# Recurrent stage and first attention tiles as one written order on each engine

## What is computed

```python
# block 1, in chunks of 64 tokens, 4 heads; state S runs over the chunks
q, k, v = x @ Wq, x @ Wk, x @ Wv
g = log_sigmoid(x @ Wgk1 @ Wgk2 + bgk2) / 16
b = cumsum(g)                        # within the chunk
A = tril((q * exp(b) * scale) @ (k * exp(-b)).T)
o = A @ v + (q * exp(b) * scale) @ S
S = S * exp(b_last) + (k * exp(b_last - b)).T @ v
y = (rmsnorm(o) * silu(x @ Wg)) @ Wo
# block 2, for each of 2 layers, 8 heads of 64, windows of 64 with one window back
q, k, v = split(shift(x) @ wqkv)
q, k = rotary(l2norm(q)), rotary(l2norm(k))
x = x + local_attention(q, k, v) @ wo
a, h = split(layernorm(shift(x)) @ w1 + b1)
x = x + (a * gelu(h)) @ w2 + b2
```

## Time and profile before

| what | value |
|---|---|
| median of 3 runs | 436.88 us (436.65 to 438.52) |
| profiled execution, device time | 436.81 us |
| its span (first to last instruction) | 435.0 us |
| busy: PE, DVE, ACT, POOL | 408.1, 338.7, 305.8, 292.5 us |
| granted TensorE clock, mean | 0.998 |

### The profile page before, as it was taken

The page is one execution under the profiler, slowest core; times in us unless marked ns, Lnnn a source line. Parts: engine busy times, 40 slices in busy tenths (PEclk is TensorE's granted clock), DMA queues, the critical chain, the costliest instruction groups (busy, mean ns, idle before and its releaser), DMA issues.

```text
span 435.0 us, 13205 instructions
## 1 busy us (share of the span) xinstructions
PE 408.1 (94%) x4851; PEld 291.9 (67%) x4851; DVE 338.7 (78%) x715; ACT 305.8 (70%) x684; POOL 292.5 (67%) x288
## 2 busy tenths in 40 slices
PE   3898999879999999999999999999999999999994
PEld 2566666656776877777765666777777777766563
DVE  2678867889988989989845277799899899855676
ACT  3677768757887887887773346778878888876324
POOL 3578967799978778777722536667767767761425
PEclk9999999999999999999999999999999999999999
DMA  7830000000000000000000000000000000000012
GB/s 188 313 91 3 2 3 3 3 1 2 8 14 10 9 10 11 8 8 14 8 9 13 0 2 1 7 10 8 11 11 8 8 15 9 8 8 12 8 36 62
DMA packets 21055, 10.37 MB, mean 24 GB/s; under 512 B 13253, under 2 KB 20225, under 8 KB 20993
## 3 DMA queue, kind: packets, MB, share of 16 engines
q1 hardware_dynamic: 20272, 9.08, 7.6%
q10 hardware_dynamic: 720, 0.46, 0.4%
HBM read 6.38 MB, written 1.05 MB: 17 GB/s over the span
## 4 chain that ended last, share of the span: by engine, by line
PE 66%; issue 7%; POOL 6%; ACT 5%; DVE 4%; POOLq 0%; ACTq 0%; DVEq 0%
PE psum L640 49%; PE psum L912 6%; PE psum L954 5%; PE psum L979 4%; ACT sq L1380 1%; PE psum L885 1%; ACT probs_t L1412 1%; POOL ping L446 1%; DVE o_n L1999 1%; POOL qr L475 1%; POOL qr L483 1%; ACT qk_t L1399 1%; DVE neg_max L1972 1%; PE psum L999 1%; POOL zn L511 1%
## 5 line engine op out<-in xcount | busy, mean ns | idle before, releaser
L475 POOL TENSOR_TENSOR qr<-rot 128x1024 f32<-128x1024 f32 x32 | 75.8, 2370 | 27.0 <-DVE rot L1944 22.2
L640 PE MATMUL psum<-wqkv_sb,h_t 128*128 128x512 f32 x192 | 93.0, 594 | 0.0
L483 POOL TENSOR_TENSOR qr<-qr,inv 128x1024 f32<-128x1024 f32 x32 | 60.9, 1902 | 33.6 <-ACT inv L1391 33.6
L1952 DVE TENSOR_REDUCE ss<-sq 128x16 f32<-128x1024 f32 x32 | 39.0, 1218 | 14.9 <-ACT sq L1380 14.7
L1405 ACT ACTIVATE probs<-probs 128x512 f32<-128x512 f32 x64 | 39.4, 631 | 13.8 <-DVE probs L1979 13.5
L1972 DVE TENSOR_REDUCE neg_max<-psum 128x4 f32<-128x512 f32 x64 | 41.5, 685 | 7.1 <-PE psum L640 5.7
L640 PE MATMUL psum<-z_t,w_sb 128*128 128x512 f32 (+1 forms) x96 | 44.7, 595 | 0.0
L640 PEld LDWEIGHTS psum<-wqkv_sb,h_t 128*128 128x128 f32 x192 | 31.7, 191 | 16.3 <-issue 16.2
L1979 DVE TENSOR_TENSOR probs<-psum,neg_max 128x512 f32<-128x512 f32 x64 | 41.3, 681 | 0.2
L1944 DVE TENSOR_TENSOR rot<-psum,cos_t 128x1024 f32<-128x1024 f32 x32 | 39.1, 1222 | 2.7 <-PE psum L640 2.4
L640 PEld LDWEIGHTS psum<-v_mix,probs_t 128*64 128x64 f32 x512 | 32.2, 137 | 12.7 <-issue 11.1
(11 more groups left out here) (155 smaller groups left out, 967.0 us busy)
## 6 DMA issues: line engine op xcount, KB each, us to landing
wqkv_sb<-in_L_ffn_wqkv SPq DMA_DIRECT2D x1, 1536.0 KB, 10.0
hcat<-middle SPq DMA_DIRECT2D x32, 32.0 KB
hcat<-middle SPq DMA_DIRECT2D x32, 31.8 KB
out_x<-pong SPq DMA_DIRECT2D x7, 128.0 KB, 1.8
x_in<-in_L_attn_x SPq DMA_DIRECT2D x2, 384.0 KB, 4.9
w_sb<-in_L_ffn_w SPq DMA_DIRECT2D x1, 682.0 KB
cos_base<-rotary_cos SPq DMA_DIRECT2D x1, 512.0 KB, 5.5
sin_base<-rotary_sin SPq DMA_DIRECT2D x1, 512.0 KB, 6.7
```

Source lines behind the costliest of these rows:

```text
L475: pool.tensor_tensor(o, a, b[:, :, ::-1, :], ALU.add).then_inc(s["add_ready"], 1)
L483: pool.tensor_tensor(a, a, inv[:, :].unsqueeze(2).to_broadcast([P, 2 * AH, DH]), ALU.mult).then_inc(s["qr_ready"], 1)
L640: return pe.matmul(o, w, m, start=start, stop=stop, skip_group_check=skip)
L1952: dve.tensor_reduce(ss[:, 0:4 * AH:2], sq[:, :].rearrange("p (h e) -> p h e", e=DH), AX.X, ALU.add).then_inc(s["ss_ready"], 1)
```

## The change

The loop `gla_step` is gone on all four compute engines, with `paired` and `FREE_PAIR`. One written list, `recurrent_stage_and_first_tiles`, holds everything from pair 0 up to where `attn_step` takes over at tile 3. Beside it:

- The combined gate weight is made in bank 7. `transpose_x(0)` no longer waits for its copy, `project_gate(0)` does.
- Pairs 0 and 1 are normalised on VectorE (`normalise_first`), not on GpSimd; pair 0 between the two copies of gate weights.
- The transposed o goes to bank 3, with one copy of 512 columns. `project_vg(t)` waits for the copy of o of pair t-2, `transpose_o(t)` for the reads of v and gate of pair t+1; `intra_outputs` no longer waits for that copy.
- Wgk1 and Wgk2 are loaded from ScalarE's queue, ahead of Wq and Wk; Wv and Wg from SP's, where the former two stood.
- The waits for `d_cols` and `zero_pool` stand in VectorE's list right before `rotate(0)`, in ScalarE's right before `copy_h_t(0)`.

```diff
@@ sync
-            sp.dma_start(wgk1_sb[:, :], Wgk1).then_inc(d["d_low"], 16)
-            sp.dma_start(wgk2_sb[0:RANK, :], Wgk2).then_inc(d["d_low"], 16)
+            sp.dma_start(wvg_sb[:, 0:GV], Wv).then_inc(d["d_vg"], 16)
+            sp.dma_start(wvg_sb[:, GV:2 * GV], Wg).then_inc(d["d_vg"], 16)
@@ tensor
-                pe.transpose(b_xg[0:RANK, 0:P], wgk1_sb[:, :], ident).then_inc(s["w1t_done"], 1)
+                pe.transpose(bank[7][0:RANK, 0:P], wgk1_sb[:, :], ident).then_inc(s["w1t_done"], 1)
                 pe.wait_ge(s["w1t_ready"], 1)
-                mm(b_xg[:, P:2 * P], wgk1_t[0:RANK, :], wgk2_sb[0:RANK, :]).then_inc(s["wgk_done"], 1)
+                mm(bank[7][:, P:2 * P], wgk1_t[0:RANK, :], wgk2_sb[0:RANK, :]).then_inc(s["wgk_done"], 1)
...
                 wait(pe, s["gin_ready"], t)
+                wait(pe, s["ogt_ready"], t - 1)
                 if t == 0:
                     pe.wait_ge(d["d_vg"], 2 * 16)
...
                 wait(pe, s["og1_ready"], t)
-                wait(pe, s["ogt_ready"], t)
...
                 wait(pe, s["og2_ready"], t + 1)
+                wait(pe, s["v_ready"], min(t + 2, NP))
+                wait(pe, s["gin_ready"], min(t + 2, NP))
                 for i in range(2 * B):
-                    ins = pe.transpose(bank[6 + i // 2][:, HC + i % 2 * P:HC + (i % 2 + 1) * P],
+                    ins = pe.transpose(bank[3][:, i * P:(i + 1) * P],
@@ vector
+            def normalise_first(t):
+
+                dve.wait_ge(s["x_rstd"], t + 1)
+                for b in range(B):
+                    at = t * B + b
+                    ins = dve.tensor_scalar(xn[:, at * P:(at + 1) * P], tile_of(x_in, at), mv_x[:, 2 * at:2 * at + 1],
+                                            rstd_x[:, at:at + 1], ALU.subtract, ALU.mult)
+                ins.then_inc(s["xn_ready"], 1)
+
             def copy_gate_weights():
 
                 dve.wait_ge(s["w1t_done"], 1)
-                dve.tensor_copy(wgk1_t[0:RANK, :], b_xg[0:RANK, 0:P]).then_inc(s["w1t_ready"], 1)
+                dve.tensor_copy(wgk1_t[0:RANK, :], bank[7][0:RANK, 0:P]).then_inc(s["w1t_ready"], 1)
+                normalise_first(0)
                 dve.wait_ge(s["wgk_done"], 1)
```

669 lines of the change are left out of this document (427 added, 242 removed).

## The result

| | before | after |
|---|---|---|
| median, same session (4 runs each) | 437.70 us (436.65 to 438.81) | 433.20 us (432.42 to 433.38) |
| profiled execution, device time | 436.81 us | 433.38 us |
| its span | 435.0 us | 431.3 us |

The ratio is 0.9888, 95% interval 0.9843 to 0.9932; timed again in another session (433.18 against 436.96 us) it is 0.9895, 0.9841 to 0.9949: about 1% less time, clear of the noise. The forecast was 433.4 us, counted from the earlier median of 436.88. Some executions of most of these kernels, the one before too, run 2 to 5 us longer at a lower granted clock (mean 0.985 to 0.994 instead of 0.995 to 0.999), which lifts some of the medians, so the gain is read from the spans (3.7 us) and such a trace is compared only in the steps before its clock falls.

The account below looks back on a forecast made before the run. TensorE's own work bounds it from 120.77 us on; before, its 16.6 us idle is all to win. A walk of the lists summed terms to 3.75, less 0.35 allowance: 3.4, so 433.4 us; 8 in 10: 430.6 to 436.9.

Parts of the forecast that it names:

- Start: Up to the first x transposition: it starts near 6.95 us instead of 7.32, +0.4, bounds 0 and 0.6.
- First two pairs: Up to vg(2): gate(1) and vg(1) fill TensorE's wait for pair 0's decays, +1.3 us.
- Pair 2: vg(2) to vg(3): costs 9.4 us, of which 0.65 for casts ahead of decay_q(2); gain 0.7.
- Pair 3: vg(3) to vg(4): costs 9.2 us, with 0.45 for second_state(3) behind decay_log(4); gain 0.4.
- Pairs 4 and 5: vg(4) to scores(6): each pair costs 8.75 us, gains 0.5 and 0.4.
- bank 3 ring: vg, copy and gate_input, o transposition, copy: 4.4 us in a pair of 8.75, hidden, free until 4 us late.
- Last pairs to the first tile: scores(6) to project_qk(0) +0.1, to transpose_qk(0) +0.35, to tile 3's scores -0.4; allowance for forgotten hand-offs -0.35 us.
- GpSimd did not hold TensorE: Rival: gate_o(7) late on GpSimd holds transpose_o(7) at tile 0, 439.1 us and more; 0.10 including other stalls.
- Waits moved: Waits for column transfers cost nothing at old or new places; the slower table is there at 17.6 us, hidden by 3.5.
- The path of o: Rival: state outputs to transpose_o has no slack, 0.45 us late in six pairs takes 2.7; 436.1 us, chance 0.16.
- The scans: Rival: all eight VectorE scans at their worst, 1.209 us, lose up to 3.0 us; 436.4 us, chance 0.06.
- More than I credit: Rival: each pair costs 8.75 us and the last stretch's five waits vanish, 2 to 3 us more; 431 us, chance 0.06.

Follow-up runs that it names:

- start undone: Changed kernel with weight queues as before, combined gate weight in bank 0, pairs 0 and 1 normalised on GpSimd; 434.43 us against 436.75 before, ratio 0.9936.
- the old order: Changed kernel, bank 3 and start edits kept, with pairs 0 to 3 in the old loop's order; 443.02 us against 436.75 before, ratio 1.0117.
- The moves above: Changed kernel with copy_h_t(2) ahead of gate_exp(7), 433.07 us; also with pair 2's scan ahead of scale_o(0) and row_reciprocals(1), normalise_o(1) ahead of row_max(2), 433.77 us.
- the mixtures tried here: Changed kernel with the old loop's order for pairs 0 to 3, 443.02 us; changed kernel with transposed o back in banks 6 and 7, 451.49 us.
- scan-first: Changed kernel with VectorE's scan of pair 2 ahead of scale_o(0); first run 432.49 us, timed 433.32 us beside 433.18 for the changed kernel.

## Why the prediction was right, and where its terms were wrong

**What bounds the kernel** was right: from tile 3's scores to the end nothing changed, and the 16.6 us of idle TensorE ahead of it were all that could be won. 3.64 of them were. The sum of the terms was forecast as 3.4, but it came right in part by luck: the start gave 1.0 us more than said and the first two pairs 0.9 less, pair 2 gave 0.6 more and pair 3 gave 0.4 less.

**Start, +0.4: mis-sized, 1.39 measured at its landmark.** The part that I had given a price (bank 7, VectorE's normalisation) gave 0.52. What I had left out stands in the trace of the kernel before, TensorE's first instruction:

```profile
5.32 0.37 PE L650 MATMUL psum<-consts,wgk_sb 128*16 128x128 f32 x1 [5.32 <-DMA wgk_sb<-in_L_attn_Wgk]
```

Its wait ended with the low-rank weights (issued from 2.11 us on by SP, now from 0.73 by ScalarE), not with the identity, and moving them was worth 0.87. I had the queue as a risk (a bound of 0), not as a gain. Wv and Wg are first used at 8.11, not after 9, and nothing waited for them.

**First two pairs, +1.3: mis-sized, 0.39.** The order did what I said, and TensorE was 1.4 us ahead of my walk at scores(0) and scores(1) (20.61 against 22.0). Then came 0.43 for copy_kd(1), which I had at 0.5, and the nameless 0.80 (by my reading the instruction block), which no walk over data dependencies shows. From scores(1) to vg(2) my walk had 6.6 us, 6.1 without its wait; measured are 7.89, 6.66 without the waits, so I had also summed the work of this piece 0.5 us too short. The two terms together were 1.7, measured 1.78: the sum was right by luck of two errors, and the experiments show that the two are linked. The start's gain is passed on in part only: 0.93 of 1.18 between the changed kernel and the one with the start undone (whose first x transposition is at 7.11), and nothing of 0.79 in the second execution of the same kernel.

**Pair 2, +0.7: 1.34.** The pair took 8.79 us; the 0.65 that I charged for the casts did not come. Their price was wrong: the earlier trace rows show the masks' cast at 1.424, but that is behind the start of a GpSimd product; here it started 0.02 us ahead of second_state(1) and took 0.35, while second_state(1) took 0.58 instead of 0.40. The scan made up for this, however: scan and casts took 2.31 us, not far below the 2.46 that I had reckoned (0.84, 1.42 and 0.2). What failed is the path. TensorE, held up in key_values(1), gave the outputs of pair 1 late, so that behind the casts VectorE had to wait for square_o(1),

```profile
28.31 0.69 DVE L1902 TENSOR_REDUCE o_ss<-z_t 128x8 f32<-128x512 f32 x1 [0.52 <-ACT z_t L1331]
```

and gate_input(2) was done at 31.80, before TensorE was free for transpose_o(1) at 31.91. With the scan moved, scan and casts took 2.58 us and the pair 8.84.

The Trainium skill, page "SBUF — State Buffer", section "SBUF: two separate sides", says that a GpSimd instruction and a VectorE instruction that uses both ports or has two SBUF inputs exclude each other for a whole instruction, and that the one that starts first goes first. The traces agree: 0.05 us behind gate_o(0) the scan took 1.75 us (0.69 when moved away), and 0.03 behind it the identity's cast took 1.32 (0.21), each ending within 0.6 us of gate_o's end.

**Pair 3, +0.4: -0.02.** I had 0.45 for second_state(3) standing behind decay_log(4); the wait is there, 0.73, but the cause that I named is wrong. GpSimd was free 0.32 us before second_state(3) started; its input came late, out of key_values(3) over state_0(3), and it took 0.71 instead of 0.40 beside VectorE's scan. Swapping it with decay_log(4) takes away the second part and costs more in the next pair, as far as one run tells.

**Pairs 4 and 5, +0.5 and +0.4: 0.44 and 0.14.** Pair 4 takes 8.78 with no wait; pair 5 has 0.26 before project_gate, for the copy of x. That the bank 3 ring is hidden was right for the new order, where no wait for it shows, but my margin of 4 us was not a property of the ring: in the old order the same ring costs 5.8 us in four places.

**Last pairs to the first tile, +0.1, +0.35, -0.4, allowance -0.35: 0.05, 0.15, -0.24.** The waits of the walk are there: 1.07 before transpose_in(3), 0.44 and 0.77 later ones, and transpose_o(7) waits only 0.17 for gate_o(7), so GpSimd did not hold TensorE. The moves above show for two of them, the 1.07 and the 0.77, that they are not gains left lying: each has a second condition close behind.

**Waits moved, 0: right** (1.0006). The tables were in time as well: cos in 5.0 us, sin in 6.2, and no wait of GpSimd on them.

**Rivals.** The path of o did not take the gain: no wait of TensorE on gate_o in each pair. The scans were worse at their worst than my bound (1.755), but their median fell (0.839 to 0.781), and VectorE's busy time ahead of tile 3 rose by 2.4 us (90.63 to 93.01), of which 1.2 are the four normalisations that it took over, so the kernel was not held by it. "More than I credit" was held off by the nameless wait in the start and by 0.73 in pair 3.

## What to carry to other kernels

Price an instruction by its row only after seeing what ran beside it on GpSimd or VectorE: the masks' cast was 1.42, 0.57 and 0.35 us here, the identity's 0.21, 0.73 and 1.32, and second_state 0.71 and 0.40. A buffer's place and the order around it are one decision: either half of this change without the other made the kernel 6 to 15 us slower, in the mixtures tried here. Before blaming the instruction ahead in an in-order list, look whether the engine idles behind it: then it is the input that is late. Before moving an instruction to remove a wait, look for the condition that ends next, on the engine that waits and on the one that gives up its filler.

## What the runs showed of the hardware that was not expected

- TensorE stands still for 0.53 to 1.63 us at one place of its instruction stream while the weights are still loading, and goes on 2.5 to 2.8 us after a 16 KB packet starts on the queue "q8 instruction" (ten traces; that the one causes the other is inferred). An earlier start of the kernel can be lost there entirely (0.79 us in one trace). What sets the start of the packet (20.75 to 22.85) stays open, and so does whether the packet is slowed by the weights.
- The granted clock falls after some of these waits and not after others. In two traces in which TensorE goes on at 25.37 and 25.43, after waits of 1.13 and 1.14, the page's clock is lower in the third of its 40 slices and vg(2) starts at 31.30 and 31.36; it doesn't fall where TensorE goes on at 25.61 after 0.81 (start undone), nor after the longest wait, 1.63. Windows of the timed scan-first trace, stretch, length, PE, PEld, DVE, ACT, POOL, PEclk, DMA:

```profile
13.70:22.80 9.10, 8.46 (x179) 5.84 (x178) 6.88 (x22) 7.74 (x22) 5.41 (x8) 1.00 1.03 381
22.80:31.36 8.56, 6.89 (x112) 5.46 (x111) 5.51 (x14) 4.74 (x13) 4.58 (x7) 0.72 0.33 58
31.36:41.20 9.84, 9.63 (x155) 6.32 (x155) 6.11 (x19) 6.29 (x20) 6.30 (x9) 0.90 0.01 2
```

A mean of 0.72 is a mix of full speed (2.4 GHz) and half (1.2 GHz); vg(2) is 2.8 us late against the second trace of the changed kernel (28.55). Of this 0.8 is the later end of the wait (25.43 against 24.64) and 2.0 the clock (5.93 us from there to vg(2) against 3.91); pair 2 costs another 1.0 (9.84 against 8.84). Together that is the 3.8 us between the two times, 437.09 and 433.32. Why the clock falls in one execution of a kernel and not in the next stays open.
